# Gating GpSimd's gathers of a Mamba stage in pairs, and the last early gathers of two expert loops two results sooner

## The reference

```python
x = x + 0.5 * ffn(layernorm(x))
x = x + attn(layernorm(x))
x = x + 0.5 * ffn(layernorm(x))

# ffn: top 4 of 16 experts by a sigmoid gate, weights normalised, plus a shared expert
h3 = silu((x @ w1_routed[e]) * (x @ w3_routed[e]));  out_e = h3 @ w2_routed[e]
ffn = silu(x @ w1_shared) * (x @ w3_shared) @ w2_shared + sum_e(weight_e * out_e)

# attn: a scan along the 512 tokens of each sequence, per channel
xp = x @ W_in.T;  dt = softplus(xp @ W_dt.T + b_dt);  a = exp(-exp(log_A) * dt)
ys[t] = a[t] * ys[t-1] + xp[t];  attn = ys @ W_out.T
```

## Time and profile before

| | us |
|---|---|
| median of 3 runs | 652.78 |
| the three runs | 653.09, 644.83, 652.78 |
| the profiled execution | 652.48 |
| its span in the profile | 650.7 |

### The profile page before, as it was taken

The page is one execution under the profiler, slowest core; times in us unless marked ns, Lnnn a source line. Parts: engine busy times, 40 slices in busy tenths (PEclk is TensorE's granted clock), DMA queues, the critical chain, the costliest instruction groups (busy, mean ns, idle before and its releaser), DMA issues.

```text
span 650.7 us, 13461 instructions
## 1 busy us (share of the span) xinstructions
PE 515.1 (79%) x3206; PEld 452.7 (70%) x3207; DVE 433.5 (67%) x1459; ACT 375.3 (58%) x1128; POOL 349.3 (54%) x364
## 2 busy tenths in 40 slices
PE   3967699999999999553776943799999999998334
PEld 3855489988889888442664932699988888887223
DVE  6889667767676767415797689477667676665425
ACT  2777466766566667543665564477666566664000
POOL 3899454456565654667011342544556565646744
PEclk9988799999999999787798975699999999999758
DMA  9961245665444454423000460254444445456524
GB/s 298 391 260 66 69 126 154 168 172 170 144 135 147 128 149 113 139 84 102 18 1 9 150 215 0 72 155 128 141 137 137 142 132 148 132 130 169 164 84 147
DMA packets 61149, 88.24 MB, mean 136 GB/s; under 512 B 9499, under 2 KB 46363, under 8 KB 61107
## 3 DMA queue, kind: packets, MB, share of 16 engines
q1 hardware_dynamic: 47379, 50.29, 22.5%
q0 software_dynamic: 13728, 37.50, 22.4%
HBM read 57.22 MB, written 30.54 MB: 135 GB/s over the span
## 4 chain that ended last, share of the span: by engine, by line
PE 53%; DVE 15%; issue 11%; ACT 9%; another core or an unknown queue 6%; DMA 4%; POOL 1%; SPq 1%; ACTq 0%; DVEq 0%; POOLq 0%
PE bank L1379 23%; PE bank L1430 10%; PE bank L1401 6%; PE bank L1441 4%; PE bank L1440 4%; PE bank L1598 2%; DVE xres L1158 2%; ACT ring_f L712 2%; ACT ring_r L663 1%; DMA ys_scratch<-ring_f 1%; ACT ring_r L672 1%; DVE lg L933 1%; PE bank L1623 1%; DMA ring_f<-xn_scratch,tokidx 1%
## 5 line engine op out<-in xcount | busy, mean ns | idle before, releaser
L558 POOL DMA_INDIRECT ring_f<-xn_scratch,tokidx x158 | 149.6, 947 | 152.7 <-PE bank L1401 96.1
L1379 PE MATMUL bank<-w_routed,ring_r 128*128 x948 | 195.2, 341 | 0.0
L1379 PEld LDWEIGHTS bank<-w_routed,ring_r 128*128 128x128 f32 x948 | 151.9, 192 | 5.3 <-issue 2.8
L1430 PE MATMUL bank<-w_routed,ring_r 128*128 x790 | 119.6, 281 | 1.8 <-ACT ring_f L691 1.1
L1430 PEld LDWEIGHTS bank<-w_routed,ring_r 128*128 128x128 f32 x790 | 110.1, 188 | 3.2 <-issue 3.2
L672 ACT ACTIVATE ring_r<-bank 128x256 fp32r<-128x256 f32 x158 | 60.6, 384 | 70.3 <-PE bank L1441 65.5
L961 DVE TENSOR_TENSOR ring_r<-bank,ring_r 128x128 fp32r<-128x128 f32 x158 | 45.5, 288 | 58.4 <-ACT ring_r L672 45.5
L594 POOL DMA_INDIRECT mamba_room<-ys_scratch,si x64 | 61.7, 964 | 29.8 <-issue 18.3
L953 DVE TENSOR_TENSOR ring_r<-bank,ring_r 128x256 fp32r<-128x256 f32 x158 | 67.1, 425 | 14.8 <-ACT ring_r L663 9.1
L1401 PE MATMUL bank<-cst,ring_f 128*128 128x128 f32 x316 | 63.9, 284 | 12.0 <-DMA ring_f<-xn_scratch,tokidx 7.4
L681 ACT ACTIVATE stage<-bank 128x176 f32<-128x176 f32 x158 | 50.4, 319 | 38.3 <-remote 16.8
(11 more groups left out here) (172 smaller groups left out, 817.1 us busy)
## 6 DMA issues: line engine op xcount, KB each, us to landing
ys_scratch<-ring_f SPq DMA_DIRECT2D x158, 128.0 KB
raw_routed<-in_w13r SPq DMA_DIRECT2D x6, 704.0 KB, 12.2
xn_scratch<-w_routed SPq DMA_DIRECT2D x32, 128.0 KB, 4.9
raw_routed<-in_w2r SPq DMA_DIRECT2D x6, 512.0 KB, 12.7
raw_routed<-in_w13r SPq DMA_DIRECT2D x8, 352.0 KB, 6.2
ring_f<-xn_scratch,tokidx POOLq DMA_INDIRECT x158
xres<-in_x_in SPq DMA_DIRECT2D x4, 512.0 KB, 6.8
raw_routed<-in_w2r SPq DMA_DIRECT2D x8, 256.0 KB, 7.1
```

The lines of the kernel that those rows point to most:

```text
L558: pool.indirect_dma_start(xg[j % UN], None, xn_dram, bass.IndirectOffsetOnAxis(ap=tokidx[:, j:j + 1], axis=0)).then_inc(s_g[j % UN], 16)
L1379: last = pe.matmul(out, a, b, start=(q == 0), stop=(q == len(terms) - 1))
L1430: last = pe.matmul(p_y[b][:, 0:D], a, v, start=(q == 0), stop=(q == 4))
```

## The change

In the Mamba stage the table of five gates per tile goes, and a table `MAMBA_DONE` of 15 products takes its place, in the order in which PE gives them. The 32 gathers are 16 pairs (two of a tile's four rows each). The first pair has no gate; pair p (1 to 15) waits for product p of the table: `xt` 1, `xp` 1, `z` 1, `xt` 2, `xp` 2, `z` 2, `xt` 3, `y` 1, `xp` 3, `z` 3, `xt` 4, `y` 2, `xp` 4, `z` 4, `xt` 5. `xp` 3 is the inputs' product of the third chunk, number 2 when counted from 0. So the first gathers of k = 2 to 5 wait for later products than before, and k = 6 and 7, which waited for DVE alone, wait for PE too. The gates are for f = 0 only.

In `fetch_early`, for both layers, n = 25 to 31 wait for a result of PE that is two earlier: n = 25 for result 71, n = 30 for 76, n = 31 for 77. The wait for a free room stays.

```diff
--- before.py
+++ after.py
@@ -42,7 +42,8 @@
 MEASURED = 5
 SCALED = ((0, 4), (4, EARLY_TILES))
 TABLE_AFTER = 76
-MAMBA_FIRST = {1: ("xt", 1), 2: ("xp", 1), 3: ("z", 1), 4: ("z", 2), 5: ("xp", 3)}
+MAMBA_DONE = (("xt", 1), ("xp", 1), ("z", 1), ("xt", 2), ("xp", 2), ("z", 2), ("xt", 3), ("y", 1), ("xp", 3), ("z", 3),
+              ("xt", 4), ("y", 2), ("xp", 4), ("z", 4), ("xt", 5))
 SH_BEFORE, SH_ENDS, SH_LAST = 1, 12, NT
 HID_AHEAD = 6
 SUMS_AFTER = {9: (0, 1), 10: (2,), 11: (3,), 12: (4,), 13: (5,), 14: (6, 7)}
@@ -568,7 +569,7 @@
                 if n >= ROWS:
                     pool.wait_ge(s_ea, f * EARLY + n - ROWS + 1)
                 if early_after(n) >= NS:
-                    pool.wait_ge(s_y, f * NS + NS - EARLY + n + 1)
+                    pool.wait_ge(s_y, f * NS + NS - EARLY + n - 1)
                 pool.indirect_dma_start(early_rows[n % ROWS], None, ys_dram[0:tiles_before(t) * P, :],
                                         bass.IndirectOffsetOnAxis(ap=si[:, n:n + 1], axis=0)
                                         ).then_inc(s_er[n % ROWS], 16)
@@ -579,9 +580,6 @@
                     pool.wait_ge(s_yw[b], written(f, b, tiles_before(t)))
                 k = t - EARLY_TILES
                 if f == 0:
-                    if k in MAMBA_FIRST:
-                        reached, chunks = MAMBA_FIRST[k]
-                        pool.wait_ge(m_s[reached], chunks)
                     if k >= ROOMS:
                         pool.wait_ge(s_cd, combined_to(f, t - ROOMS))
                 elif k >= 2:
@@ -590,6 +588,9 @@
                         pool.wait_ge(s_cd, combined_to(f, t - 3))
                 for q in range(TOPK):
                     n = t * TOPK + q
+                    if f == 0 and q % 2 == 0 and 2 * k + q // 2 >= 1:
+                        reached, chunks = MAMBA_DONE[2 * k + q // 2 - 1]
+                        pool.wait_ge(m_s[reached], chunks)
                     room = cgl[t - EARLY_TILES] if f else cg[(t - EARLY_TILES) % ROOMS]
                     pool.indirect_dma_start(room[:, q, :], None, ys_dram[0:tiles_before(t) * P, :],
                                             bass.IndirectOffsetOnAxis(ap=si[:, n:n + 1], axis=0)
```

## The result

| | before | after |
|---|---|---|
| median of 20 runs, us | 651.77 | 645.90 |
| ratio, 95% interval | | 0.9927 [0.9901, 0.9953] |
| the profiled execution, its span | 652.48, 650.7 | 644.02, 642.2 |

The change makes the kernel 0.73% faster, 4.8 us (3.1 to 6.5) by the ratio: small, but the interval excludes no change. The ratio goes by the fast runs alone: a run over 1.5% above the fastest of its kernel, as one of 990.82 us of the kernel before, is left out. The forecast was 643, or 8.9 us less.

A forecast was written before the change was run, and what follows sets the result against it. PE's signals were taken to be held while POOL issues gathers back to back. Gains of 7.6 us in the Mamba stage and 1.25 in the tail, 8.9 together, took 652.5 to 643.6, stated as 643; range 631 to 653.

The forecast's parts named there:

- The reading of "remote": Mamba stage, loops, tail: PE's signals are held while POOL issues gathers one after another, 11.7 us at longest, until it stops.
- Case (b): Whole kernel: holds have another cause or only change place, so only the tail's 1.25 us is left; 651 us, 19%.
- four terms: Mamba stage: gains of 2.7, 7.5 and 0.9 us less 3.5 us given back, 7.6 us in all.
- step 3: Mamba stage, inputs' product of chunk 1 to chunk 2's: first hold nearly unchanged (0.3 us), next product 2.7 us sooner.
- step 4: Mamba stage, inputs' product of chunk 2 to chunk 3's: undisturbed, 7.7 us as before.
- step 5: Mamba stage, inputs' product of chunk 3 to chunk 4's: hold of 4.2 us instead of 11.7, gaining 7.5 us.
- step 6: Mamba stage, from chunk 4's inputs' product: late gathers now run beside it, giving back 0 to 7 us, taken as 3.5.
- The 0.9 us in the sum: Mamba stage: a gain of 0.9 us, estimated from a shorter pause saving time by a faster clock.
- case (a): Mamba stage and tail: spacing the gathers cures the holds altogether; 632 us, 28%.
- The release: After POOL stops, held PE signals come through 0.85 us later, the loop's value; 1.1 and 2.95 us were also seen.
- Case (c): Mamba stage: each gate pays for its own late signal, POOL's normalising of chunk 6 is late; 665 us, 8%.
- this reaches the end: Tail: its first gather starts 1.25 us sooner (0 to 2.4), shortening the kernel because POOL's gathers and the hold bind it.

## Why the prediction was right, and where its steps were not

**The reading of "remote" was right in its main half.** On the held chips PE's signals came late beside POOL's gathers in a row, 11.7 us in the longest hold of the Mamba stage of before. It was an inference from neighbours in time; three runs now show it, each by one profile, by taking away the gathers (71.3 us, no such wait), their issuer together with their queue (72.2, none) or their closeness (none). Case (b), that the holds have another cause, has fallen; its other half, that they only change place, is part of what happened. The second half of the reading, that the signals come through when POOL stops, is too simple: long holds ended 1.1 to 4.1 us behind a stop, or in one case after 15 us without one (at 615.63, before). And in the profile after the inputs' product of chunk 1 was copied without delay at 277.50, while POOL issued 12 gathers in a row. What neither the profile of before nor my list of cases had in it is that the chip decides: on the chip of 591 us the same instructions at the same spacing of 1.25 us leave no wait on "remote" in any of the four profiles, and there the parts of the change and its opposite, no gates, all lie within 0.2% of before.

**That the gates gave the gain** rests on exclusion. Alone they are at 0.9966 [0.9929, 1.0002], an interval that includes 1. But the early gathers alone are at 0.9998 [0.9959, 1.0037], and both measurements of the changed kernel, [0.9901, 0.9953] and [0.9836, 0.9895], lie below that interval, if chips of the held kind may be set side by side. On the chip of 659 us no gates, the five gates, and the 15 with the early gathers stand in this order: 1.0049, 1, 0.9865.

**The sum for the stage.** I had 7.6 us out of four terms. The profile of after has 10.7, the ratio of 20 runs says 4.8 for the whole change where I had 8.9, and a second chip 8.9. So the size was right within what chips and executions differ by, but the terms were not, and that their sum came near is in part luck. I walked the pairs against the holds as they fell in one execution. I expected the hold on the inputs of chunk 1 to stay; it was gone (step 3 took 8.5 us, not 14.2). I expected step 4 undisturbed and step 5 with a hold of 4.2; it was the other way round, 13.3 and 6.7 us, where I had named 10 to 14 for step 5 as a mark to look for. I expected 0 to 7 us to be given back beside step 6, and found 4.2 (11.5 against 7.3), near the 3.5 that I took. The 0.9 us in the sum was my estimate of what a shorter pause saves by a faster clock, and no run shows it: pauses of 4.45 and 3.96 us were each followed by a product as slow (3.78 and 3.67 us) as the one behind the pause of 12.36. POOL's stops were to be near 280, 283 and 300, and were at 271.0 and 286.6. The step that failed is to take a hold as something with a place. Which of the signals beside gathers in a row is held, the runs don't show. In the working itself, five pairs of 2.5 us from 266.41 end near 278.6 and not 279.3, which would have ended that hold some 0.7 us sooner, and 643.6 was put down as 643.

**That most gates are open** was right and is the limit of the change. From 289.84 POOL put out 16 gathers without a stop, and PE's pause of 3.96 us in step 6 fell among them. So case (a), 632 us, was not reached with gates on PE; a stage of 71 us was seen on a held chip only with a quarter of POOL's gathers, or with none.

**The release.** I took 0.85 us from the loop for all stops. At 289.84, POOL itself had stood 3.20 us at a gate for a product that had ended at 282.68, like the 2.95 of before. The 0.85 was the shortest of the releases that I had.

**The gathers' end** was to be 312, and was 311.48. That nobody waits for a row was right. Case (c) wanted pauses of 1.6 us at 15 gates before PE waits for POOL; the kernel with 16 pauses of 1 us has PE waiting 5.34 us. It came sooner than I worked out. The shorter holds pull the normalising forward, which I had counted against the loss and not in the threshold: in the profile after, the 20 us of slack were already 7.4.

**Gathers as early as can be** gained nothing. They have slack, 20.17 us at the end of POOL's 32 in the profile of before, and on a held chip the kernel without gates is 3.2 us slower (1.4 to 5.0). On the other kind of chip leaving out the gates made no difference of more than 0.45% either way.

**The early gathers.** The step up to the tail's start was right to the digit: 1.22 us behind PE's last result and not 2.48. The step "this reaches the end" is not borne out: alone, this part is at 0.9998, and the tail of the changed kernel's profile is longer by 2.7 us. The waits of 15 us in it, against a gain of 1.25, are a likely reason, which no run tested. The 1.25 us stay unshown, in either sense.

## What to carry to other kernels

When an engine idles on a signal whose sender had long ended, look at what POOL issues at that time, and try a stop of about 1 us in its stream of indirect DMAs, or another issuer, before moving any work. Look at long waits marked "issue" too. A gate on the consumer's progress makes POOL stop only while POOL is ahead (in the changed kernel 16 gathers went out without a stop from 289.84); once it is behind, only a pause of its own does, and its price is what waits at the end of POOL's queue (PE's 5.34 us in the kernel with pauses). Compare on more than one chip: the kernel before took 648 to 659 us on three chips, where every profile has waits on "remote", and 591 us on another, where no profile of the four has one.

## What the runs showed of the hardware

- On the held chips signals of PE arrived late beside POOL's indirect DMAs of 128 rows every 1.25 us: 11.7 us late in the Mamba stage of before, 15.9 us of idling there without gates. In the tails of the held chips the longest wait on "remote" was from 8.6 us (early gathers alone) to 24.7 (changed, chip of 659 us). A signal of DVE in the same time was not late: in the long hold of before ACT took up at 299.97 what DVE had ended at 299.93 (timelines of both). On the chip of 591 us, with the same stream, no engine waited on "remote" in any of four profiles.
- As many transfers of 128 KB issued by SP, 32 in 29.5 us with breaks of 1 us and more between fours, left no wait on "remote" in the Mamba stage.
- Stops of 0.97 us (one of 1.44) after each two gathers were enough for there to be no wait on "remote" in the Mamba stage. In the loops, three gathers in a row with a stop of about 1.2 us left waits of up to 2.0 us. On the held chips the first loop took 188.7 to 192.1 us against 170.5 to 172.8 on the other, the second 186.3 to 190.5 against 168.6 to 170.4.
- Which part of the chip or its set-up makes this difference, the runs don't show.
